# Softmax maxima carried by small DMAs and heads turned by VectorE, in a four-layer hybrid network

## The chip, the cores and the metric

One core of a Trainium2 chip runs the whole network in one launch. The metric is the device time of one execution in microseconds (us). The engines are TensorE (PE), which multiplies matrices and, with an identity, transposes; VectorE (DVE); ScalarE (ACT); GpSimd (POOL); and SyncE (SP), which here only issues DMAs. SBUF is the working memory of 128 partitions, PSUM the eight banks that TensorE writes.

## The reference

Sixteen images of 256 tokens and 128 channels pass four layers; all is float32. The change touches the second, and the first half of the third:

```
# L1: dense attention, 8 heads of D=16 (per image, 256 queries x 256 keys)
attn = softmax(einsum('bihd,bjhd->bijh', q, k) * D**-0.5, axis=2)
x = einsum('bijh,bjhd->bihd', attn, v).reshape(bs, n, 128) @ W_last.T + b_last + x
# L2: on layer-normed tokens, key j counts for query i where i-64 < j <= i
scores = where(valid, einsum('bnqd,bnkd->...', q, k) / sqrt(D), -1e30)
t = t + (softmax(scores) @ v).reshape(B, S, 128) @ Wo.T
t = t + experts(ln(t))        # top 2 of 16, mean form
```

Before them stands a spatial and channel gate (L0), after them a causal linear attention and experts with top 1 of 8 (L3).

## The kernel before

`attend` (L365) does both attentions in one loop. A tile n is one image: tiles 0 to 15 are dense, 16 to 31 windowed. A tile has four steps j=0 to 3, a step is two heads of one parity (the two heads that share a block of 32 partitions differ in parity, and the keys are kept in an even and an odd copy, in which the other head's 16 rows are zero). So there are 128 steps, s=4n+j. All engines walk the same steps, each in its own written order, and semaphores tie them; nothing is reordered by a scheduler.

In step s TensorE runs `by_query(s)` (L569): scores with queries on partitions, into one pair of PSUM banks. VectorE's `maximum(s)` (L832) takes each query's negated row maximum from them. The next by_query overwrites the banks and so waits for `max_ready`; in a windowed tile `mask_scores` (L616) goes ahead of it and waits. Five steps later (LAG), t=s-5, TensorE makes the scores again with keys on partitions (`by_key(t)`, L586), ScalarE takes the exponential (L755) into `prob`, and in windowed tiles GpSimd cuts out what lies outside the window (L496, L500). `weigh` (L639) multiplies with the values at j=1 and j=3 of a later tile; a column of ones in the values gives the softmax sums.

How the maximum comes to the other orientation: at j=3 VectorE's `split_max` (L846, L848) writes a tile's maxima as a high and a low part into `parts`, TensorE turns them at the next j=0 (`turn_max`, L624), ScalarE copies them (`take_max`, L748), and in each later step four matmuls `less_maximum` (L578) add them to the key scores:

```
for block in blocks:
    for i in range(2): less_maximum(i, block)   # pick x maxT, start=True
    for i in range(2): mm = by_key(i, block)    # start=False, stop=True
```

How the heads come out: ScalarE copies them from PSUM (`take_heads`, L762), TensorE turns them at j=0 (`turn_heads`, L652, four transposes), VectorE divides at j=1 (L854 reciprocal, L860 twice), TensorE turns back at j=2 (`turn_normed`, L659), ScalarE copies (`take_normed`, L769), and TensorE applies the output weight at the next j=0 (`project_out`, L668). VectorE adds the residual (`add_out`, L870) and measures the rows for the layer norm (L876, L882). Other work in the steps: `project` (L535) makes the next tile's queries and keys at j=2; ScalarE takes the query (L733, L736) and the even key (L741), VectorE the odd key (`take_odd`, L807); `project_v` (L544) and `take_values` (L822, L824) make the values; `turn_rows` (L676) and `gate_logits` (L688) serve the layers after. VectorE's expert choice (`choose`, L1553 and after) runs in steps of the last tiles. SyncE writes finished windowed rows to a table (L472).

Of the kernel before, what the change touches and what calls it, by code (L numbers as in the profile page):

```python
# [364 lines left out]
def attend(nc, xf, tokens, rows, table, weights, consts, q_bias, key_scales, v_bias, o_bias, pick, window_mask, gate,  # L365
# [22 lines left out]
    with stage(nc, "attend") as (sb, sem):  # L388
        query = sb("query", [128, 3, N])
        key = sb("key", [128, 3, 2, N])  # L390
        negmax = sb("negmax", [128, 2, 2, 4, 2])
        parts = sb("parts", [128, 2, 128], FP32R)
        maxT = sb("maxT", [128, 2, N], FP32R)
        vaug = sb("vaug", [128, 3, 2, 2, 4, 32])
        prob = sb("prob", [128, 2, 4, 2 * 512])
        heads = sb("heads", [128, 2, 2, 128])
        recip = sb("recip", [128, 16])
        normed = sb("normed", [128, 2, 128])
# [20 lines left out]
        high_max = sem("high_max")  # L419
        parts_ready = sem("parts_ready")  # L420
        max_turned = sem("max_turned")
        maxT_ready = sem("maxT_ready")
# [5 lines left out]
        heads_ready = sem("heads_ready")  # L428
# [3 lines left out]
        normed_turned = sem("normed_turned")  # L432
# [31 lines left out]

        with nc.Block() as block:
            @block.sync
            def _(sp):
                sp.wait_ge(zero_row_set, 1)
                sp.dma_start(table[0:1, :], zero_row[:]).then_inc(table_written, 16)
                for k in range(IMAGES):  # L470
                    sp.wait_ge(rows_ready, IMAGES + k + 1)
                    sp.dma_start(table[1 + N * k:1 + N * (k + 1), :].rearrange("(a p) c -> p a c", p=128),  # L472
                                 rows[:, 2 * k:2 * k + 2, 0:C]).then_inc(table_written, 16)
                sp.wait_ge(table_written, 16 * (IMAGES + 1))

            @block.gpsimd
            def _(pool):
                nc.gpsimd.memset(zero_row[:], 0.0).then_inc(zero_row_set, 1)
                nc.gpsimd.memset(parts[:].bitcast(FP32), 0.0).then_inc(zeros_set, 1)
# [44 lines left out]
            def _(pe):  # L524
                def project(n):
                    if n >= 1:
                        pe.wait_ge(query_ready, n)
                        pe.wait_ge(odd_ready, n)
                    if windowed(n):
                        pe.wait_ge(rowsT_ready, n - IMAGES + 1)  # L530
                        pe.wait_ge(vaug_ready, n)
# [18 lines left out]
                def score_pairs(s):  # L550
# [13 lines left out]
                    def by_query(i, piece):  # L564
# [4 lines left out]
                        return nc.tensor.matmul(ps[:, SCORE + i, at:at + width], query[rows, n % 3, a * 128:(a + 1) * 128],  # L569
                                                key[rows, n % 3, odd, from_:from_ + width], start=not windowed(n),  # L570
                                                stop=not windowed(n) or a == 1)

                    def less_maximum(i, block):
                        n, m = t // 4, t % 4
                        groups, odd = tiles(m)
                        rows = slice(32 * groups[i], 32 * groups[i] + 32)
                        b, from_, width, at = block
                        nc.tensor.matmul(ps[:, KEY_SCORE + i, at:at + width], pick[rows, odd, :],  # L578
                                         maxT[rows, n % 2, from_:from_ + width], start=True, stop=False)

                    def by_key(i, block):
# [6 lines left out]
                                                query[rows, n % 3, from_:from_ + width], start=False, stop=True)  # L588
# [30 lines left out]
                def turn_max(n):  # L619
                    pe.wait_ge(parts_ready, n + 1)  # L620
                    if n - 6 >= IMAGES:
                        pe.wait_ge(logits_taken, n - 5 - IMAGES)
                    for a in range(2):
                        mm = nc.tensor.transpose(ps[:, MISC, a * 128:(a + 1) * 128], parts[:, a].bitcast(FP32), ident)  # L624
                    mm.then_inc(max_turned, 1)

                def weigh(n, g):
                    if g == 0:
                        pe.wait_ge(vaug_ready, n + 1)
                        if n >= 1:  # L630
                            pe.wait_ge(heads_ready, n)
# [11 lines left out]

                def turn_heads(n):
# [1823 lines left out]
```

## Time and profile before

| | us |
|---|---|
| median of 3 runs | 893.64 (893.03 to 894.1) |
| profiled execution, its own time | 893.71 |
| its span | 892.0 |
| TensorE busy | 735.9 (83%) |
| VectorE busy | 606.4 (68%) |
| ScalarE busy | 422.3 (47%) |
| GpSimd busy | 421.5 (47%) |

The span runs from the first to the last record of the profiled execution; the execution's own time holds a little more around it. Busy shares are means over the whole network, which has stages with different limits; the stage in question runs from by_query at 79 us to about 453. A row of the timeline is one instruction, or several alike in a row (x4: from the first one's start to the last one's end); rows can overlap, since matmuls are pipelined and those on different blocks of 32 partitions run beside each other.

### The profile page before, as it was taken

What the parts mean: (1) busy time and instruction counts of PE and PEld (TensorE: products, weight loads), DVE (VectorE), ACT (ScalarE), POOL (GpSimd) and SP (SyncE); (2) the same over time, 40 slices, a digit from 0 to 9 for tenths busy, and PEclk for the clock granted to TensorE, in tenths of its full rate; (3) what the DMA queues carried; (4) which work ended last, traced back from release to release, by engine and by line L of the source; (5) the groups of instructions that cost most, each with busy time, mean ns of one, the idle gap of its engine ahead of it and who ended that gap; (6) DMA issues with size and microseconds to landing.
All of it is one profiled execution on the core that took longest, in us unless ns stands there. A gap on an engine that the chain in (4) does not pass through costs nothing. (4 is left out here: it accounts for less than half of the span.)

```text
span 892.0 us, 22133 instructions
## 1 busy us (share of the span) xinstructions
PE 735.9 (83%) x7941; PEld 571.1 (64%) x7941; DVE 606.4 (68%) x1583; ACT 422.3 (47%) x861; POOL 421.5 (47%) x560
## 2 busy tenths in 40 slices
PE   0659899999999999999864898866699888539994
PEld 0235566666667777777653787854467666439993
DVE  3765667777766666677469888867557777647774
ACT  0454555555554444444344566650466666124442
POOL 0336012222226776766820777730555687825551
PEclk9979999999999999999875899996799999659996
DMA  5830000000000000000000111140700000122216
GB/s 170 253 124 1 1 2 1 2 3 1 2 3 1 3 19 14 14 14 14 19 13 3 49 54 55 52 27 0 217 2 2 8 17 20 40 72 74 62 50 189
DMA packets 38222, 37.19 MB, mean 42 GB/s; under 512 B 4851, under 2 KB 30440, under 8 KB 38116
## 3 DMA queue, kind: packets, MB, share of 16 engines
q1 hardware_dynamic: 31204, 24.28, 9.2%
q0 software_dynamic: 4800, 9.40, 4.5%
q10 hardware_dynamic: 2112, 2.10, 0.7%
q8 instruction: 66, 1.08, 0.5%
q14 instruction: 40, 0.33, 0.1%
HBM read 26.76 MB, written 9.46 MB: 41 GB/s over the span
## 5 line engine op out<-in xcount | busy, mean ns | idle before, releaser
L832 DVE TENSOR_REDUCE attend_negmax<-ps 128x4 f32<-128x1024 f32 (+1 forms) x128 | 139.8, 1092 | 91.3 <-PE ps L569 90.8
L755 ACT ACTIVATE attend_prob<-ps 128x1024 f32<-128x1024 f32 (+1 forms) x128 | 110.6, 864 | 160.3 <-PE ps L586 160.0
L569 PE MATMUL ps<-attend_key,attend_query 32*128 32x256 f32 (+2 forms) x1024 | 124.8, 360 | 7.5 <-DVE attend_negmax L832 7.4
L586 PE MATMUL ps<-attend_query,attend_key 32*128 32x256 f32 (+2 forms) x1024 | 127.1, 343 | 0.0
L569 PEld LDWEIGHTS ps<-attend_key,attend_query 32*128 32x128 f32 x1024 | 79.5, 184 | 48.1 <-issue 46.4
L1817 POOL DMA_INDIRECT sums_xs<-table,sums_source x79 | 77.1, 976 | 56.8 <-DVE sums_source L1750 33.0
L578 PE MATMUL ps<-attend_maxT,pick 32*128 32x256 f32 (+2 forms) x512 | 100.2, 387 | 0.5 <-ACT attend_prob L755 0.5
L1535 PE MATMUL ps<-sums_xT,sums_own 128*128 128x128 f32 x632 | 84.2, 280 | 0.0
L1535 PEld LDWEIGHTS ps<-sums_xT,sums_own 128*128 128x128 f32 x632 | 78.5, 195 | 0.0
L586 PEld LDWEIGHTS ps<-attend_query,attend_key 32*128 32x128 f32 x1024 | 77.9, 185 | 0.3
L506 POOL TENSOR_SCALAR attend_rstd<-attend_spread 128x2 f32<-128x2 f32 x32 | 7.4, 231 | 142.5 <-DVE attend_spread L882 142.5
L1878 ACT ACTIVATE sums_hidden<-ps 128x512 f32<-128x512 f32 x79 | 47.2, 598 | 34.9 <-PE ps L1535 33.5
L496 POOL TENSOR_SCALAR_AFFINE_SELECT attend_prob<-attend_prob 128x512 f32<-128x512 f32 x64 | 41.0, 641 | 45.9 <-ACT attend_prob L755 45.9
L2050 POOL DMA_INDIRECT outputs<-expert_y,expert_token x39 | 37.9, 971 | 49.0 <-DVE expert_y L2156 45.1
L639 PE MATMUL ps<-attend_prob,attend_vaug 128*32 128x256 f32 (+2 forms) x1024 | 58.3, 345 | 0.6 <-POOL attend_prob L500 0.6
L1888 DVE TENSOR_REDUCE partial<-sums_hidden 128x4 f32<-128x512 f32 x79 | 53.9, 682 | 5.6 <-ACT sums_hidden L1878 2.3
L1282 ACT ACTIVATE linear_prob<-ps 128x1536 f32<-128x1536 f32 x32 | 46.2, 1443 | 16.6 <-PE ps L1150 16.6
L513 POOL TENSOR_SCALAR rows<-tokens,attend_spread,attend_rstd 128x128 f32<-128x128 f32 x64 | 50.7, 801 | 3.3
L578 PEld LDWEIGHTS ps<-attend_maxT,pick 32*128 32x128 f32 x512 | 47.9, 183 | 1.6 <-ACT attend_prob L755 1.4
L1083 POOL TENSOR_SCALAR_AFFINE_SELECT linear_prob<-linear_prob 128x1024 f32<-128x1024 f32 x32 | 35.0, 1094 | 28.0 <-ACT linear_prob L1282 27.9
L1524 DVE COPY sums_own<-w1T 128x512 f32 x79 | 34.6, 438 | 16.3 <-PE ps L1535 10.5
L2141 ACT ACTIVATE expert_hidden<-expert_before 128x512 f32<-128x512 f32 x39 | 24.6, 630 | 41.8 <-DVE expert_before L2182 41.8
(356 smaller groups left out, 1764.2 us busy)
## 6 DMA issues: line engine op xcount, KB each, us to landing
w<-in_L_ffn_w SPq DMA_DIRECT2D x1, 4096.0 KB, 27.7
expert_xs<-slots SPq DMA_DIRECT2D x39, 64.5 KB, 1.8
x<-in_x ACTq DMA_DIRECT2D x4, 512.0 KB, 8.0
table<-rows SPq DMA_DIRECT2D x16, 128.0 KB
experts<-in_L_ffn_W SPq DMA_DIRECT2D x1, 2048.0 KB, 8.5
experts<-in_L_ffn_W SPq DMA_DIRECT2D x4, 512.0 KB, 10.3
rows<-outputs SPq DMA_DIRECT2D x8, 256.0 KB, 5.1
out<-expert_result SPq DMA_DIRECT2D x8, 256.0 KB, 2.6
```

Of the source, the lines that this page charges most:

```text
L513: last = nc.gpsimd.tensor_scalar(rows[:, t, 0:C], tokens[:, t, :], spread[:, n % 2, a, 0:1], rstd[:, n % 2, a:a + 1], ALU.subtract, ALU.mult)
L569: return nc.tensor.matmul(ps[:, SCORE + i, at:at + width], query[rows, n % 3, a * 128:(a + 1) * 128], key[rows, n % 3, odd, from_:from_ + ...
L578: nc.tensor.matmul(ps[:, KEY_SCORE + i, at:at + width], pick[rows, odd, :], maxT[rows, n % 2, from_:from_ + width], start=True, stop=False)
L586: return nc.tensor.matmul(ps[:, KEY_SCORE + i, at:at + width], key[rows, n % 3, odd, b * 128:(b + 1) * 128], query[rows, n % 3, from_:from ...
L639: mm = nc.tensor.matmul(ps[32 * r:32 * r + 32, HEADS, c:c + width], vaug[:, n % 3, b, g, r, :], of_pair(n, 2 * g + r // 2)[:, r % 2, at:at ...
L755: nc.scalar.activation(of_pair(t // 4, t % 4)[:, :, 0:wide], ps[:, KEY_SCORE:KEY_SCORE + 2, 0:wide], ACT.Exp).then_inc(prob_ready, 1)
L832: last = nc.vector.tensor_reduce(out=negmax[:, s // 4 % 2, :, r:r + 2, odd].rearrange("p a r -> p r a"), in_=ps[:, SCORE:SCORE + 2, 0:2 * ...
L1282: nc.scalar.activation(prob[:, s % 2, :, 0:384], ps[:, SCORE:SCORE + 4, 0:384], ACT.Copy).then_inc(prob_ready, 1)
L1535: mm = nc.tensor.matmul(ps[:, bank + r % 2, c * 128:(c + 1) * 128], own[:, r % ring, c * 128:(c + 1) * 128], xT[:, r % 4, :], start=True, ...
L1817: nc.gpsimd.indirect_dma_start(out=xs[:, s % RING, :], out_offset=None, in_=table[:, :], in_offset=bass.IndirectOffsetOnAxis(ap=source[:, ...
L1878: nc.scalar.activation(hidden[:, r % 2, :], ps[:, UP + r % 2, :], ACT.Silu).then_inc(hidden_ready, 1)
L1888: nc.vector.tensor_reduce(out=partial[:, bass.ds(s, 1), :].rearrange("p s c -> p (s c)"), in_=hidden[:, r % 2, :].rearrange("p (c n) -> p ...
```

## The change

Two things change in `attend`, and one in how its keys are taken.

The maxima. The query is now held twice (`query[128, 3, 2, N]`), once per parity, with the other parity's 16 rows zero. Of these 16 unused rows one is used to carry the negated maximum, and the key's matching row holds 1, set by a bias as the key is taken; by_key then gives scores less maximum in one product, and less_maximum is gone. To get a maximum into that row, VectorE turns each step's four columns of maxima in 32x32 blocks (`turn_max(s)`, each step, after the step's other VectorE work), and SyncE moves them with four DMAs of 1x4x32 numbers (`place_max(s)`). by_key waits for `max_placed`. When by_query reads the same copy, before its maximum exists, that row still holds the zeros with which the query was taken.

The heads. VectorE turns them from PSUM in 32x32 blocks (`turn_heads`, j=0), inverts the sums (j=1), multiplies (`normalise`, one operation on two SBUF tiles, j=2) and turns back (`turn_normed`, j=3). TensorE's and ScalarE's parts of this are gone.

The odd key is taken by ScalarE. Waits follow: `project` waits for `vaug_ready` from tile 1 on, `turn_rows` for `rowsT_ready`.

```diff
@block.sync
-                for k in range(IMAGES):
+                def place_max(s):
+                    n, m = s // 4, s % 4
+                    groups, odd = tiles(m)
+                    sp.wait_ge(max_turned, s + 1)
+                    for i in range(2):
+                        row = free_row(groups[i], odd)      # 32 * group + 16 * (1 - odd)
+                        for a in range(2):
+                            sp.dma_start(query[row:row + 1, n % 3, odd, a * 128:(a + 1) * 128],
+                                         negmaxT[2 * a + i::32, s % 4, :]).then_inc(max_placed[s % 4], 16)
...
+                for s in range(4 * (COUNT + 7)):
+                    if s < SLOTS:
+                        place_max(s)
+                    if s % 4 == 0 and IMAGES <= s // 4 - 6 < COUNT:
+                        write_rows(s // 4 - 6 - IMAGES)
@block.tensor
-                        if t % 4 == 0:
-                            pe.wait_ge(maxT_ready, t // 4 + 1)
+                        pe.wait_ge(max_placed[t % 4], 64 * (t // 4 + 1))
                         if t >= 1:
                             pe.wait_ge(prob_ready, t)
                         for block in blocks:
-                            for i in range(2):
-                                less_maximum(i, block)
                             for i in range(2):
                                 mm = by_key(i, block)
@block.scalar
+                    for odd in range(2):
+                        took = nc.scalar.activation(query[:, n % 3, odd, :], ps[:, PROJECT, 0:N], ACT.Identity,
+                                                    scale=query_scale[:, odd:odd + 1],
+                                                    bias=query_scale[:, 2 + odd:3 + odd])
...
                     if j == 3 and runs(n + 1):
                         take_query(n + 1)
                         take_even(n + 1)
+                        take_odd(n + 1)
@block.vector
+                def turn_max(s):
+                    dve.wait_ge(max_ready, s + 1)
+                    if s >= 4:
+                        dve.wait_ge(max_placed[s % 4], 64 * (s // 4))
+                    nc.vector.transpose(negmaxT[:, s % 4, :], negmax[:, s % 2, :]).then_inc(max_turned, 1)
+
+                def turn_heads(n):
+                    dve.wait_ge(weighted, 2 * n + 2)
...
+                    nc.vector.transpose(headsT[:].rearrange("p g k d -> p (g k d)"), ps[:, HEADS, :])\
+                        .then_inc(heads_turned, 1)
...
+                    nc.vector.tensor_tensor(normed[:].rearrange("p k (g d) -> p g k d", g=2), headsT[:, :, :, 0:16],
+                                            recip[:, :, :, None].to_broadcast([128, 2, 8, 16]), ALU.mult)\
+                        .then_inc(normed_ready, 1)
```

On TensorE, in a dense tile in the middle of the run, steps j=1 and j=2 stand so before (L569 by_query, L578 less_maximum, L586 by_key, L639 weigh, L535 project, L676 turn_rows, L659 turn_normed):

```order
L569 MATMUL ps<-attend_key,attend_query 128x256 x4
L578 MATMUL ps<-attend_maxT,pick 128x256 x2
L586 MATMUL ps<-attend_query,attend_key 128x256 x2
L578 MATMUL ps<-attend_maxT,pick 128x256 x2
L586 MATMUL ps<-attend_query,attend_key 128x256 x2
L639 MATMUL ps<-attend_prob,attend_vaug 32x256 x8
L569 MATMUL ps<-attend_key,attend_query 128x256 x4
L578 MATMUL ps<-attend_maxT,pick 128x256 x2
L586 MATMUL ps<-attend_query,attend_key 128x256 x2
L578 MATMUL ps<-attend_maxT,pick 128x256 x2
L586 MATMUL ps<-attend_query,attend_key 128x256 x2
L535 MATMUL ps<-xf,wqk 128x256 x2
```

And so afterwards, from j=0 to j=2 (L586 is now by_query, L596 by_key, L561 project_v, L649 project_out, L638 weigh, L552 project, L658 turn_rows):

```order
L586 MATMUL ps<-attend_key,attend_query 128x256 x4
L596 MATMUL ps<-attend_query,attend_key 128x256 x4
L561 MATMUL ps<-wv,xf 128x128 x2
L649 MATMUL ps<-wo,attend_normedT 128x128 x2
L586 MATMUL ps<-attend_key,attend_query 128x256 x4
L596 MATMUL ps<-attend_query,attend_key 128x256 x4
L638 MATMUL ps<-attend_prob,attend_vaug 32x256 x8
L586 MATMUL ps<-attend_key,attend_query 128x256 x4
L596 MATMUL ps<-attend_query,attend_key 128x256 x4
L552 MATMUL ps<-xf,wqk 128x256 x2
L658 MATMUL ps<-const_all,rows 128x128 x2
```

The four less_maximum matmuls are gone from each step and no transpose of heads is left; the rest keeps its place.

On VectorE the same tile from j=1 to j=3 before (L832 maximum, L854 and L860 the division, L876 and L882 the row measures, L846 and L848 split_max, L807 take_odd):

```order
L832 TENSOR_REDUCE attend_negmax<-ps 128x2x2
L854 RECIPROCAL attend_recip<-ps 128x16
L860 TENSOR_TENSOR attend_normed<-ps,attend_recip 128x2x4x16 x2
L832 TENSOR_REDUCE attend_negmax<-ps 128x2x2
L876 BN_STATS attend_stats<-tokens 128x6 x2
L882 BN_AGGR attend_spread<-attend_stats 128x2 x2
L832 TENSOR_REDUCE attend_negmax<-ps 128x2x2
L846 CAST attend_parts<-attend_negmax 128x8x2
L848 TENSOR_TENSOR attend_parts<-attend_negmax,attend_parts 128x8x2
L807 TENSOR_SCALAR attend_key<-ps,key_scale 128x256
```

And afterwards from j=2 to j=0 (L782 maximum, L809 normalise, L831 and L837 the row measures, L792 turn_max, L817 turn_normed, L798 turn_heads, L825 add_out):

```order
L782 TENSOR_REDUCE attend_negmax<-ps 128x2x2
L809 TENSOR_TENSOR attend_normed<-attend_headsT,attend_recip 128x2x8x16
L831 BN_STATS attend_stats<-tokens 128x6 x2
L837 BN_AGGR attend_spread<-attend_stats 128x2 x2
L792 STREAM_TRANSPOSE attend_negmaxT<-attend_negmax 128x32
L782 TENSOR_REDUCE attend_negmax<-ps 128x2x2
L817 STREAM_TRANSPOSE attend_normedT<-attend_normed 128x256
L792 STREAM_TRANSPOSE attend_negmaxT<-attend_negmax 128x32
L782 TENSOR_REDUCE attend_negmax<-ps 128x2x2
L798 STREAM_TRANSPOSE attend_headsT<-ps 128x512
L825 TENSOR_TENSOR tokens<-tokens,ps 128x256
L792 STREAM_TRANSPOSE attend_negmaxT<-attend_negmax 128x32
```

The division moved from j=1 to j=2, ahead of the row measures, and each step ends with a transpose between its own maximum and the next.

## Rows read from the trace of the kernel before

**Rows 1.** Stretches: start:end, us, busy (instructions) by engine, clock, DMA share, GB/s.

```profile
92.90:103.00 10.10, 7.64 (x93) 5.48 (x92) 6.26 (x10) 6.33 (x9) 0.00 (x0) 1.00 0.00 0
150.12:161.12 11.00, 10.63 (x137) 7.57 (x135) 7.91 (x18) 6.34 (x10) 2.53 (x4) 1.00 0.01 1
```

**Rows 2.** Timeline, TensorE, dense tile: start, duration, engine, line, out<-in [idle before].

```profile
154.19 0.48 PE L569 MATMUL ps<-attend_key,attend_query 32*128 32x256 f32 x2 [0.19 <-DVE attend_negmax L832]
...
156.68 0.60 PE L652 MATMUL ps<-const_all,attend_heads 128*128 128x128 f32 x4
...
159.79 0.48 PE L569 MATMUL ps<-attend_key,attend_query 32*128 32x256 f32 x2 [0.18 <-DVE attend_negmax L832]
...
162.30 0.38 PE L659 MATMUL ps<-const_all,attend_normed 128*128 128x128 f32 x2
```

**Rows 3.** Timeline, TensorE and VectorE, a dense step early in the stage.

```profile
94.13 1.23 DVE L832 TENSOR_REDUCE attend_negmax<-ps 128x4 f32<-128x1024 f32 x1 [0.61 <-PE ps L569]
...
95.50 0.48 PE L569 MATMUL ps<-attend_key,attend_query 32*128 32x256 f32 x2 [1.12 <-DVE attend_negmax L832]
...
96.68 1.23 DVE L832 TENSOR_REDUCE attend_negmax<-ps 128x4 f32<-128x1024 f32 x1 [1.32 <-PE ps L569]
```

**Rows 4.** Timeline, ScalarE, the even key in that dense tile.

```profile
162.66 0.56 ACT L741 ACTIVATE attend_key<-ps,key_scale 128x256 f32<-128x256 f32 x1
```

**Rows 5.** Timeline, all engines, a windowed tile's steps j=2 and j=3.

```profile
292.13 0.38 PE L569 MATMUL ps<-attend_key,attend_query 32*128 32x128 f32 x2
...
293.02 0.96 DVE L832 TENSOR_REDUCE attend_negmax<-ps 128x4 f32<-128x768 f32 x1 [0.70 <-PE ps L569]
...
294.04 0.64 POOL L496 TENSOR_SCALAR_AFFINE_SELECT attend_prob<-attend_prob 128x512 f32<-128x512 f32 x1 [1.00 <-ACT attend_prob L755]
...
294.94 0.38 PE L569 MATMUL ps<-attend_key,attend_query 32*128 32x128 f32 x2
...
297.28 0.38 PE L569 MATMUL ps<-attend_key,attend_query 32*128 32x128 f32 x2
```

**Rows 6.** Timeline, TensorE: first windowed step, last step, last weigh, last project_out.

```profile
253.60 0.38 PE L569 MATMUL ps<-attend_key,attend_query 32*128 32x128 f32 x2
...
424.25 0.38 PE L569 MATMUL ps<-attend_key,attend_query 32*128 32x128 f32 x2
...
439.58 0.75 PE L639 MATMUL ps<-attend_prob,attend_vaug 128*32 128x192 f32 x16 [0.65 <-POOL attend_prob L500]
...
445.01 1.22 PE L668 MATMUL ps<-wo,attend_normedT 128*128 128x128 f32 x4 [0.80 <-ACT attend_normedT L769]
```

**Rows 7.** VectorE groups by line: shapes, count | busy us, mean ns | idle before.

```profile
L1888 DVE TENSOR_REDUCE partial<-sums_hidden 128x4 f32<-128x512 f32 x79 | 53.9, 682 | 5.6 <-ACT sums_hidden L1878 2.3
...
L870 DVE TENSOR_TENSOR tokens<-tokens,ps 128x256 f32<-128x256 f32 x32 | 13.2, 412 | 9.7 <-PE ps L668 9.7
...
L1555 DVE TENSOR_TENSOR choice_scratch<-choice_scratch,const_all 128x128 f32<-128x128 f32 x8 | 2.2, 279 | 0.2
```

**Rows 8.** Timeline, VectorE and GpSimd: row measures, and split_max beside a select.

```profile
151.11 0.48 DVE L876 BATCH_NORM_STATS2 attend_stats<-tokens 128x6 f32<-128x128 f32 x2
151.62 0.25 DVE L882 BATCH_NORM_AGGREGATE attend_spread<-attend_stats 128x2 f32<-128x6 f32 x2
...
296.85 0.65 POOL L496 TENSOR_SCALAR_AFFINE_SELECT attend_prob<-attend_prob 128x512 f32<-128x512 f32 x1 [1.47 <-ACT attend_prob L755]
...
297.04 0.49 DVE L848 TENSOR_TENSOR attend_parts<-attend_negmax,attend_parts 128x16 fp32r<-128x16 f32 x1
```

**Rows 9.** One line's instructions: count, shortest/median/longest ns, first and last start.

```profile
L848 DVE TENSOR_TENSOR attend_parts<-attend_negmax,attend_parts x32: 175/243/490, 90.2 to 426.3; 128x16 fp32r<-128x16 f32 x32
```

**Rows 10.** Timeline, SyncE's DMA issues at the kernel's start.

```profile
2.20 0.75 SPq L2297 DMA_DIRECT2D w_wv_r<-in_L_conv_wv_r  x1
...
12.23 0.43 SPq L2312 DMA_DIRECT2D gate_bias<-in_L_ffn_bs  x1
```

**Rows 11.** DMA issues by name: count, KB each, median us to landing.

```profile
expert_xs<-slots SPq DMA_DIRECT2D x39, 64.5 KB, 1.8
```

More of the change, by code:

```diff
@@ L418, in attend @@
         max_ready = sem("max_ready")
-        high_max = sem("high_max")
-        parts_ready = sem("parts_ready")
         max_turned = sem("max_turned")
-        maxT_ready = sem("maxT_ready")
+        max_placed = [sem(f"max_placed{r}") for r in range(4)]
         key_scored = sem("key_scored")
@@ L463, in tiles, with free_row @@
             return (2 * (m % 2), 2 * (m % 2) + 1), m // 2
+        def free_row(group, odd):
+            return 32 * group + 16 * (1 - odd)
         with nc.Block() as block:
@@ L568, in by_query @@
                         a, from_, width, at = piece
-                        return nc.tensor.matmul(ps[:, SCORE + i, at:at + width], query[rows, n % 3, a * 128:(a + 1) * 128],
+                        return nc.tensor.matmul(ps[:, SCORE + i, at:at + width],
+                                                query[rows, n % 3, odd, a * 128:(a + 1) * 128],
                                                 key[rows, n % 3, odd, from_:from_ + width], start=not windowed(n),
                                                 stop=not windowed(n) or a == 1)
[L573 to L579, printed above, removed]
                     def by_key(i, block):
@@ L587, in by_key @@
                                                 key[rows, n % 3, odd, b * 128:(b + 1) * 128],
-                                                query[rows, n % 3, from_:from_ + width], start=False, stop=True)
+                                                query[rows, n % 3, odd, from_:from_ + width], start=True, stop=True)
                     pieces, blocks = PIECES[windowed(s // 4)], BLOCKS[windowed(t // 4)]
@@ L617, in mask_scores @@
                                              window_mask[:, 128:512], start=True, stop=False)
[L619 to L625, printed above, removed]
                 def weigh(n, g):
@@ L701, in _ @@
                     if j == 0:
-                        if runs(n - 1):
-                            turn_max(n - 1)
                         if runs(n):
@@ L707, in _ @@
                             project_out(n - 4)
-                        if runs(n - 3):
-                            turn_heads(n - 3)
                     if j == 1 and runs(n - 2):
@@ L718, in _ @@
                             turn_rows(n - 5)
-                        if runs(n - 3):
-                            turn_normed(n - 3)
                     if j == 3 and runs(n - 2):
@@ L784, in _ @@
                 take_even(0)
+                take_odd(0)
                 for s in range(4 * (COUNT + 7)):
                     n, j = s // 4, s % 4
-                    if j == 0 and runs(n - 3):
-                        take_heads(n - 3)
                     if j == 3 and runs(n + 1):
```

179 lines of the change are left out of this document (66 added, 113 removed).

## The prediction

> **What bounds the kernel now.** I read first the stretches of the attention stage, engine by engine. In one dense tile of 11.00 us TensorE is busy 10.63, VectorE 7.91, ScalarE 6.34 [rows 1]; in a tile's length at the start, when weigh, turn_heads and turn_normed do not run yet, TensorE is busy 7.64 of 10.10 at granted clock 1.00 [rows 1]. So TensorE is full in the steady state, and what leaves it can count, until something else is full.
>
> What comes next is read in the timeline. There is one pair of score banks, so by_query (L569) of a step waits for the row maximum (L832) of the step before. Where TensorE has nothing more to do, this loop is seen alone: by_query at 95.50, maximum at 96.68 (1.18 later) for 1.23, and by_query 0.14 after a maximum's end (94.13+1.23=95.36, then 95.50) [rows 3]. That is 2.55 a step, and the two maxima stand 2.55 apart. Four steps are 10.20; the tile takes 11.00 because step j=0, where turn_heads starts 2.49 after by_query (154.19, 156.68) and runs 0.60, and j=2, where turn_normed starts 2.51 after by_query (159.79, 162.30) and runs 0.38, stand beyond 2.55 [rows 2]. Those tails are what this change removes.
>
> In the windowed half the loop is shorter: by_query to maximum 0.89 (292.13, 293.02), maximum 0.96, and the mask matmuls before the next by_query. Step j=3 took 2.34 (294.94, 297.28), step j=2, which TensorE overfills, 2.81 (292.13, 294.94) [rows 5].
>
> **The change, term by term.** All sums go against the profiled execution: 893.71 us, its span 892.0 and 1.7 around it; the median 893.64 is 0.07 below, which I ignore.
>
> *Dense steps.* From the seventh by_query (95.50) to the first windowed one (253.60) there are 58 steps in 158.10 us [rows 3, 6], 2.73 each. TensorE loses less_maximum in all steps, turn_max and turn_heads in j=0, turn_normed in j=2. Even with the others left in, j=0 ends at 2.49 and j=2 at 2.51 [rows 2]; both are below 2.55, so the loop is the floor, unless VectorE overfills it.
>
> VectorE may work 2.55-1.23=1.32 between two maxima. No row shows a 32x32-block transpose. The nearest row reads 128x512 in one pass in 0.682 (L1888) [rows 7]. As bounds I set one half, 0.34, and double, 1.36, and take 0.68, since the tile has that row's size. For the 128x32 turn_max I take 0.18, the shortest L848, with its longest, 0.49, as bound [rows 9]. Step j=0 is then 0.68+0.41 (add_out, L870 [rows 7])+0.18=1.27 and fits. In j=1, take_values and the reciprocal are at most 0.41+0.41+0.25 by larger rows [rows 7, 8], with turn_max 1.25: fits. In j=2 stand normalise, one operation of L870's size, 0.41, the row measures 0.76 (151.11 to 151.62+0.25 [rows 8]), turn_max 0.18 and 0.06 of gaps: 1.41, that is 0.09 over. In j=3 a 128x256 transpose of at most 0.68 fits. A tile is 10.20+0.09=10.29, a step 2.57: 58 x 2.57=149.2. **Gain 8.9.**
>
> ScalarE gains a second query and the odd key, 0.56 each at most like the even key at 162.66 [rows 4]. With them the exponential of j=3 starts at 162.66+3x0.56=164.34 and ends 1.02 later at 165.36; by_query of the next j=0 would start at 159.79+5.19=164.98, and by_key stands 0.25 behind it. So by_key is at worst 0.13 late, in a step whose TensorE work is the 2.49 less turn_max and less_maximum. I cost it at nothing; if that cover is gone it is 0.13 in each tile, 4 us.
>
> *Windowed steps.* 63 steps from 253.60 to 424.25 take 170.65 [rows 6]. I take j=1 and j=3 as 2.34, j=0 as 2.44 (its mask has the wide form, whose weight load stands before it; by the rows it lies between 2.34 and 2.81). VectorE's room is 2.34-0.96=1.38 and 1.48; the 1.27 and 1.25 fit. In j=2 something new collides. GpSimd's causal select starts 1.91 after by_query (294.04) and runs 0.64 [rows 5]; the maximum ends at 0.89+0.96=1.85, and normalise, which now reads two SBUF tiles instead of PSUM and SBUF, starts there. The trace shows what then happens: L848, two SBUF inputs, takes 0.18 at best but 0.49 at 297.04, while GpSimd's select runs from 296.85 to 297.50 [rows 8, 9]. I take a stall of 0.54, between nothing and the select's whole 0.65: the step is 1.85+0.54+0.41+0.76+0.18-0.89=2.85. A tile is 2.44+2.34+2.85+2.34=9.97; sixteen less the last step are 157.2. In about five tiles the expert choice adds an operation of 0.28 (L1555 [rows 7]) to each step, which no longer all fits: 0.5 a tile, 2.4. Together 159.6: **gain 11.0.**
>
> The Trainium skill, *SBUF — State Buffer*, section "Who interferes with whom", states that a VectorE instruction with two SBUF inputs and a GpSimd instruction that reads SBUF hold each other up, the later one waiting until the first is through. It speaks against this change, since normalise did not fall under it before; the trace agrees (0.18 and 0.49). By it step j=2 stays near 2.85; without it the step would be 2.44 and the total some 6 us lower, near 865.
>
> *Drain.* After the last weigh (439.58+0.75=440.33) project_out starts at 445.01, 4.68 later [rows 6], through two engines' changes for each turn. Afterwards there are VectorE's 0.68, 0.25, 0.41 and at most 0.41 in a row, and some 0.75 of hand-overs: 2.5. **Gain 2.2.** The stage's start, where the first steps have no keys to compute, I take as even.
>
> *What is added at nothing.* SyncE issues four DMAs a step, 512 in all, and by_key waits for their landing. Its twenty issues from 2.20 to 12.23 stand 0.53 apart [rows 10]; four are 2.11, below the shortest step, 2.34. The maximum is used five steps later: 5x2.34=11.7 after by_query; 2.2 to 2.9 go until it is turned, 2.1 into issuing, so over 6 us remain for landing, against 1.8 in the nearest row [rows 11] and bounds of nothing and some three times that. The rows of windowed tiles written to HBM share that queue, one DMA in four steps, 0.53 more; the slack above covers it.
>
> Sum: 8.9+11.0+2.2=22.1, **871.5 us**; without neighbours' cases the forecast's own range is 865 to 880 (transposes up to 0.9, a stall of 0 to 0.65).
>
> The Trainium skill, *Vector Engine (DVE) Microarchitecture Reference*, §3.8 "The reshape front-end and per-opcode configuration", states that the transpose is pipelined to one element per cycle and lane. No run here shows it yet; by it the dear case below falls away and the sum stands.
>
> **The rivals.**
>
> *Dear transposes.* If a block transpose takes two passes, turn_heads is 1.36 and j=0 on VectorE 1.95, 0.63 over in the dense half: the tile is 10.20+0.63+0.09=10.92, a step 2.73, gain 0. In the windowed half 0.47 a tile more, 7.5: gain 3.5; drain 1.2. Total 889. For it: no row shows the operation. Against: nothing in the rows makes one pass over such a tile dearer than 0.68.
>
> *Slower: SyncE cannot feed the maxima.* Each step needs four issues in order. At the longest row, 0.75 and 0.04 to the next [rows 10], a step takes 3.16; the 121 steps from 95.50 to 424.25 take 382 instead of 328.75, plus 53: 947. It decides from 328.75/121/4=0.68 an issue. The late form is landing: beyond some 6 us, each microsecond delays one in five steps' worth, about 24 us over 121 steps. For it: 0.53 is not far from 0.59, where it would use up a 2.34 step. Against: the small copies in the rows all start within 0.8 of each other.
>
> *The clock.* TensorE gets more gaps. Rows 1 show 76% busy at clock 1.00, and the tile afterwards is no emptier, since it has weigh in it. If the clock did fall to 1.2 GHz, 7.64 of work would be 15.3, 5 us more in a tile; the gain is gone after four of 32 tiles.
>
> *TensorE stays full.* If the matmul timings in the records hide more than they show, j=0 and j=2 keep their length; then only the drain is gained: 888 to 895. Against: the 2.49 and 2.51 are starts of instructions.
>
> *Better.* No stall and a shorter loop: 860 to 865.
>
> **How the numbers follow.** Forecast (865 to 880) 0.66; dear transposes 0.13; SyncE slower 0.10; clock 0.03; TensorE full 0.04; better 0.04. A measurement of this kernel tells about 0.2% from no change, 1.8 us. Faster: 0.66+0.04+most of the dear case, 0.12=0.82; the rest of that case and of the full TensorE are the 0.06 within; slower 0.12. The range reaches from 863 to 890, over the forecast, half of "better" and most of the dear case; the slower one lies outside.
>
> **What would show it.** By_query starts 2.55 apart in dense tiles, 10.2 to 10.4 a tile; VectorE's transposes at most 0.7 (128x512) and 0.2 (128x32); TensorE near 85% busy in a tile and the releaser of its gaps the maximum, not the DMA; in windowed j=2 a normalise near 0.95 instead of 0.41; SyncE's queue under 90% busy and by_key never released by a DMA; 2.5 from the last weigh to project_out. I am wrong if by_key waits for max_placed, if a dense tile stays near 11, or if the span outside the stage moves.

## The result

The changed kernel takes 865.54 us (median of 4, 864.95 to 866.61) against 893.66 for the kernel before in the same runs; the ratio is 0.9687, 95% interval 0.967 to 0.9704. It is 28.1 us faster; 22.1 were predicted (871.5, range 863 to 890). Its profiled execution took 864.95, the span 863.2.

Where the span's 28.8 us went, by landmarks of both traces (VectorE's maxima, and TensorE's first matmul of the next stage):

| stretch | before | after | gain | predicted |
|---|---|---|---|---|
| to the first maximum | 80.23 | 80.95 | -0.7 | 0 |
| 64 dense steps, to the first windowed maximum | 174.26 | 162.64 | 11.6 | 8.9 (of 58 steps) |
| 63 windowed steps, to the last maximum | 170.65 | 152.40 | 18.3 | 11.0 |
| drain, to the next stage | 28.47 | 28.54 | -0.1 | 2.2 |
| the rest | 438.39 | 438.67 | -0.3 | 0 |

VectorE's groups after the change, by shape (x count | busy us, mean ns | idle before); they answer to [rows 7, 9]:

```profile
L792 DVE STREAM_TRANSPOSE attend_negmaxT<-attend_negmax 128x32 f32<-128x32 f32 x128 | 22.8, 178 | 0.3
L798 DVE STREAM_TRANSPOSE attend_headsT<-ps 128x512 f32<-128x512 f32 x32 | 22.6, 706 | 5.8 <-PE ps L638 5.8
L817 DVE STREAM_TRANSPOSE attend_normedT<-attend_normed 128x256 f32<-128x256 f32 x32 | 13.9, 434 | 0.0
L809 DVE TENSOR_TENSOR attend_normed<-attend_headsT,attend_recip 128x256 f32<-128x256 f32 x32 | 13.7, 429 | 0.0
```

The transposes cost 0.178, 0.434 and 0.706, where 0.18, at most 0.68, and 0.68 were taken. From 256 to 512 columns the price rises by 0.272, 1.06 ns a column (the source also changes, from SBUF to PSUM). A row maximum, one pass over PSUM, rises by as much: 0.692 for 128x512 (in half_max below) and 1.224 for 128x1024 are 1.04 ns a column. The Trainium skill, *Vector Engine (DVE) Microarchitecture Reference*, §3.8 "The reshape front-end and per-opcode configuration", states one element per cycle and lane for the transpose; a price per column that equals a one-pass operation's agrees with that.

A dense tile of after, as in [rows 1, 3]: the stretch, then VectorE's maxima and TensorE's by_query (L586) in the timeline:

```profile
142.57:152.66 10.09, 9.50 (x114) 6.48 (x110) 8.08 (x19) 6.19 (x9) 2.53 (x4) 1.00 0.01 2
```

```profile
142.57 1.22 DVE L782 TENSOR_REDUCE attend_negmax<-ps 128x4 f32<-128x1024 f32 x1 [0.88 <-PE ps L586]
...
143.85 0.48 PE L586 MATMUL ps<-attend_key,attend_query 32*128 32x256 f32 x2
...
145.06 1.22 DVE L782 TENSOR_REDUCE attend_negmax<-ps 128x4 f32<-128x1024 f32 x1 [0.21 <-PE ps L586]
...
146.43 0.48 PE L586 MATMUL ps<-attend_key,attend_query 32*128 32x256 f32 x2 [0.25 <-DVE attend_negmax L782]
...
147.60 1.23 DVE L782 TENSOR_REDUCE attend_negmax<-ps 128x4 f32<-128x1024 f32 x1 [0.70 <-PE ps L586]
...
148.91 0.48 PE L586 MATMUL ps<-attend_key,attend_query 32*128 32x256 f32 x2
...
150.11 1.22 DVE L782 TENSOR_REDUCE attend_negmax<-ps 128x4 f32<-128x1024 f32 x1 [0.18 <-PE ps L586]
```

The tile is 10.09 instead of 11.00, at clock 1.00. Its steps from j=0 to j=3, by the maxima, are 2.49, 2.54, 2.51, 2.55. In j=1 TensorE waits for the maximum (0.25), in j=3 too (0.34 before 151.48); in j=0 and j=2 it hardly does, by_query follows 0.06 and 0.08 after the maximum's recorded end. So the loop is the floor of j=1 and j=3, and TensorE's own work, just as long, that of j=0 and j=2; half_max_odd below shows that part. TensorE's busy time, 9.50, is 94% of the tile and not the expected 85%. Records of matmuls overlap, and how much of the 9.50 is due to that no run here tells.

In windowed tiles the steps are 2.34 all round, except j=2, 2.37 in tiles 17 to 21 and 2.77 from tile 22, where gate_logits joins TensorE's j=2 (before: 2.81 and 3.21).

### The profile page after: what moved, and what is told of

The parts are those of the page before. It is cut to its first block and busy times, and to the rows that moved or that the text cites. A ratio compares the mean times of both kernels' runs of the same rounds, so it can differ in the third digit from the quotient of the medians.

```text
span 863.2 us, 21250 instructions
## 1 busy us (share of the span) xinstructions
PE 688.5 (80%) x7173; PEld 521.9 (60%) x7173; DVE 612.1 (71%) x1648; ACT 418.2 (48%) x829; POOL 424.5 (49%) x560
## 5 line engine op out<-in xcount | busy, mean ns | idle before, releaser
L782 DVE TENSOR_REDUCE attend_negmax<-ps 128x4 f32<-128x1024 f32 (+1 forms) x128 | 139.6, 1090 | 82.9 <-PE ps L586 82.2
L729 ACT ACTIVATE attend_prob<-ps 128x1024 f32<-128x1024 f32 (+1 forms) x128 | 110.7, 865 | 137.2 <-PE ps L596 137.2
L586 PE MATMUL ps<-attend_key,attend_query 32*128 32x256 f32 (+2 forms) x1024 | 124.8, 360 | 12.8 <-DVE attend_negmax L782 11.6
L596 PE MATMUL ps<-attend_query,attend_key 32*128 32x256 f32 (+2 forms) x1024 | 124.6, 359 | 1.1 <-ACT attend_prob L729 1.0
L586 PEld LDWEIGHTS ps<-attend_key,attend_query 32*128 32x128 f32 x1024 | 79.6, 184 | 53.5 <-issue 45.7
L596 PEld LDWEIGHTS ps<-attend_query,attend_key 32*128 32x128 f32 x1024 | 88.3, 184 | 2.3 <-issue 2.2
L638 PE MATMUL ps<-attend_prob,attend_vaug 128*32 128x256 f32 (+2 forms) x1024 | 58.8, 348 | 0.7 <-POOL attend_prob L516 0.6
L512 POOL TENSOR_SCALAR_AFFINE_SELECT attend_prob<-attend_prob 128x512 f32<-128x512 f32 x64 | 45.0, 702 | 24.7 <-ACT attend_prob L729 24.7
L516 POOL TENSOR_SCALAR_AFFINE_SELECT attend_prob<-attend_prob 128x512 f32<-128x512 f32 x64 | 40.8, 637 | 4.4
L1495 PE MATMUL ps<-expert_xT,expert_own 128*128 128x128 f32 x312 | 42.4, 280 | 0.0
```

Source lines behind the costliest of these rows:

```text
L512: nc.gpsimd.affine_select(out=causal, in_=causal, pattern=[[0, 2], [0, 2], [1, 128]], base=0, channel_multiplier=-1, compare_op=ALU.is_ge, ...
L596: return nc.tensor.matmul(ps[:, KEY_SCORE + i, at:at + width], key[rows, n % 3, odd, b * 128:(b + 1) * 128], query[rows, n % 3, odd, from_ ...
L638: mm = nc.tensor.matmul(ps[32 * r:32 * r + 32, HEADS, c:c + width], vaug[:, n % 3, b, g, r, :], of_pair(n, 2 * g + r // 2)[:, r % 2, at:at ...
L729: nc.scalar.activation(of_pair(t // 4, t % 4)[:, :, 0:wide], ps[:, KEY_SCORE:KEY_SCORE + 2, 0:wide], ACT.Exp).then_inc(prob_ready, 1)
L782: last = nc.vector.tensor_reduce(out=negmax[:, s % 2, 0:4].rearrange("p (a r) -> p r a", a=2), in_=ps[:, SCORE:SCORE + 2, 0:2 * width].rea ...
L1495: mm = nc.tensor.matmul(ps[:, bank + r % 2, c * 128:(c + 1) * 128], own[:, r % ring, c * 128:(c + 1) * 128], xT[:, r % 4, :], start=True, ...
```

## The experiments

The diffs are shortened to the lines that carry the change; some comments in them are mine. Those of heads_alone and maxima_alone are shown against the kernel before.

**Each part alone.** `heads_alone` is the kernel before with the heads' new way and the odd key on ScalarE; `maxima_alone` is the changed kernel with the heads' old way.

```diff
# heads_alone
-                        if runs(n - 3): turn_heads(n - 3)     # TensorE, j=0; turn_normed, j=2; ScalarE's copies
+                        if runs(n - 3): turn_heads(n - 3)     # VectorE, j=0; normalise j=2, turn_normed j=3
# maxima_alone
-                            for i in range(2): less_maximum(i, block)
+                        pe.wait_ge(max_placed[t % 4], 64 * (t // 4 + 1))
```

> The heads' way of the change (and the odd key on ScalarE), with the maxima's old way: split_max, turn_max, take_max and less_maximum stay. Theory (the loop of by_query and maximum is the floor, and each part alone clears most of what stood above it): steps j=0 go from 3.05 to about 2.55 in dense tiles and from 3.01 to about 2.5 in windowed ones, j=2 from 2.85 to 2.55 and from 2.81 to 2.55 (late windowed tiles 3.21 to 2.95); about 10 us in the dense half and 12 in the windowed one: 871. The rival, that the time follows TensorE's busy time: six transposes a tile are 0.98 us of matmul records against 3.1 for less_maximum (100.2 us in 32 tiles), so a quarter of the gain: 887.

> The maxima's way of the change (and the odd key on ScalarE), with the heads' old way: take_heads, six transposes on TensorE, two take_normed copies stay. Theory of the floor: less_maximum is worth about 0.25 us of a step's length and turn_max 0.27, so j=0 goes from 3.05 to about 2.53 and j=2 from 2.85 to 2.6, windowed alike: 871, and with the run of the heads alone the two gains add up to far more than the whole change's 28. The rival (busy time): three quarters of the gain, 872, but then the heads alone give 887 and the gains add up.

Measured: 880.15 (ratio 0.9838, 0.9809 to 0.9868) and 878.26 (0.9837, 0.9797 to 0.9877), gains of 13.5 and 15.4. Both expectations missed. That the two add up to 28.9, the whole change's 28, is partly chance, since the steps do not add up. By the maxima, steps j=0 and j=2 in dense tiles are 2.62 and 2.78 with the heads alone, 2.75 and 2.73 with the maxima alone, 2.49 and 2.51 with both: each part alone leaves TensorE above the loop's floor, and only both together bring it down to it. From 3.05, j=0 gains 0.43 by the heads, 0.30 by the maxima and 0.56 by both; from 2.85, j=2 gains 0.07, 0.12 and 0.34. Where heads_alone loses time, in the timeline around the start of a step j=2 (L568 by_query, L577 less_maximum, L534 project):

```profile
177.86 1.02 ACT L733 ACTIVATE attend_prob<-ps 128x1024 f32<-128x1024 f32 x1 [1.50 <-PE ps L585]
```

```profile
178.76 0.48 PE L568 MATMUL ps<-attend_key,attend_query 32*128 32x256 f32 x2
178.94 0.39 PE L577 MATMUL ps<-attend_maxT,pick 32*128 32x256 f32 x2
...
180.24 1.13 PE L534 MATMUL ps<-xf,wqk 128*128 128x256 f32 x4
...
181.52 0.48 PE L568 MATMUL ps<-attend_key,attend_query 32*128 32x256 f32 x2
```

The exponential ends at 178.88, and less_maximum starts 0.06 later, 0.18 behind by_query (0.03 in the kernel before); project then starts 1.48 after by_query instead of 1.33. There is one pair of key-score banks too, and with less_maximum in it this second loop is 2.52 long. I tested that by a shorter exponential:

```diff
# heads_half_exp
-                    wide = WIDE[windowed(t // 4)]
+                    wide = 256 if 8 <= t < 4 * IMAGES else WIDE[windowed(t // 4)]
```

> The heads alone, and in the dense tiles (from step 8 on) the exponential is taken of half of each head's key scores, so the outputs are not the reference's. In the run of the heads alone j=2 stayed at 2.78 where 2.55 was expected. Theory: there is a second loop, by_key to exponential to the next by_key, over the one pair of key-score banks; with less_maximum in it, it is 1.44+1.02+0.06=2.52, so by_key starts 0.18 behind by_query and project 0.17 later than in the kernel before. With an exponential of half the size (0.5 less) that delay goes: project at 1.33 after by_query instead of 1.50, j=2 2.61, total some 2 us below the heads alone. The rival, that the transposes left more on TensorE than their starts showed: 2.78 and the same total.

Measured: 875.6 (0.9802, 0.9785 to 0.9819), 4.5 below the heads alone where 2 was expected. Steps j=2 fell from 2.78 to 2.63, windowed ones stayed; by_query, less_maximum and project now stand so:

```profile
167.92 0.48 PE L568 MATMUL ps<-attend_key,attend_query 32*128 32x256 f32 x2 [0.18 <-DVE attend_negmax L792]
167.95 0.39 PE L577 MATMUL ps<-attend_maxT,pick 32*128 32x256 f32 x2
...
169.25 1.13 PE L534 MATMUL ps<-xf,wqk 128*128 128x256 f32 x4
```

0.03 and 1.33, as expected: the second loop is shown, and it is 0.15 of the 0.27 that j=2 loses when less_maximum goes too (2.78 to 2.51). The steps explain only some 2 of the 4.5: the dense steps take 2.0 less, but the first maximum of tile 28 stands at 369.24 instead of 370.76, since the stage began 0.4 later, and the rest lies behind this stage and stays open. With half the exponential the later layers work on other numbers.

**The loop after.** `half_max` shortens the maximum, `half_max_odd` also takes the odd key back to VectorE, `odd_on_vector` does only that.

```diff
# half_max: dense tiles
-   in_=ps[:, SCORE:SCORE + 2, 0:2 * width].rearrange("p r (a n) -> p r a n", a=2),
+   in_=ps[...].rearrange("p r (a n) -> p r a n", a=2)[:, :, :, 0:width if windowed(s // 4) else width // 2],
# odd_on_vector: ScalarE's take_odd(n + 1) goes; VectorE at j=3, behind turn_normed
+                        if runs(n + 1): take_odd(n + 1)
```

> The changed kernel; in the dense tiles VectorE takes the maximum over the first 128 of the 256 keys only, so what is subtracted is not the true maximum. Theory (after the change the loop of by_query and maximum is the floor of j=1 and j=3, 2.54, and TensorE's own work, 2.48, that of j=0 and j=2): a maximum of 0.68 instead of 1.22 frees j=1 and j=3 to about 2.3 and leaves j=0 and j=2, a dense tile goes from 10.09 to 9.55, total 857.5. The rival, that SyncE's DMAs or the exponential hold the steps: 865.5.

> The changed kernel with the odd key back on VectorE, at j=3 behind turn_normed. Theory (it is on no path: 0.53 fits into VectorE's room at j=3, 1.2 to 1.4 with 0.6 in it): 865.5 within 1. The rival, that ScalarE's longer j=3 holds by_key up, or that VectorE has no room: 3 us off in either direction.

> Half the maximum in dense tiles as in the run before, with the odd key back on VectorE. With half the maximum a dense tile fell to 9.91 only, since j=0 rose to 2.94: by_key waits there for the exponential of j=3, which stands behind two queries and two keys on ScalarE. Theory: with the odd key gone from ScalarE that exponential is 0.45 earlier, j=0 falls to about 2.5 and a tile to 9.5, total 856 to 858. The rival, that VectorE or SyncE holds j=0: 862.

Measured: odd_on_vector 866.1 (0.9695, 0.9671 to 0.9719), no difference, so that edit is free in the changed kernel. half_max 862.19 (0.9662, 0.9645 to 0.9678): j=1 and j=3 fell to 2.26 and 2.09, so the maximum did hold them, but j=0 rose to 2.94 and the tile stood at 9.91. Why, in half_max's timeline at the end of j=3 and the start of j=0 (L716, L721 the keys, L729 the exponential, L586 by_query, L596 by_key):

```profile
177.54 0.56 ACT L716 ACTIVATE attend_key<-ps,key_scale 128x256 f32<-128x256 f32 x1
...
177.99 0.57 ACT L721 ACTIVATE attend_key<-ps,key_scale 128x256 f32<-128x256 f32 x1
...
178.44 1.03 ACT L729 ACTIVATE attend_prob<-ps 128x1024 f32<-128x1024 f32 x1
...
178.83 1.13 PE L586 MATMUL ps<-attend_key,attend_query 32*128 32x256 f32 x8
...
179.62 1.13 PE L596 MATMUL ps<-attend_query,attend_key 32*128 32x256 f32 x8
```

by_key waits 0.79 behind by_query for an exponential that stood behind the keys. half_max_odd confirms it: 856.24 (0.9568, 0.9543 to 0.9592), j=0 2.55, a tile 9.52, as expected. There TensorE has no gap left, over 10 us of dense tiles (us, busy of PE, PEld, DVE, ACT, POOL, clock):

```profile
130.00:140.00 10.00, 10.00 (x115) 7.04 (x116) 7.05 (x22) 6.28 (x9) 2.53 (x4) 1.00 0.01 1
```

So 9.5 a tile is TensorE's own work, and the changed kernel's 10.09 stands 0.6 above it for the maximum's sake. ScalarE's cover for the odd key, costed at nothing, is real but only as wide as the loop is long.

**SyncE's DMAs.**

```diff
# fifth_dma, behind the four of place_max
+                    sp.dma_start(spare[0:1, s % 4, :], negmaxT[4:128:32, s % 4, :]).then_inc(max_placed[s % 4], 16)
-                        pe.wait_ge(max_placed[t % 4], 64 * (t // 4 + 1))
+                        pe.wait_ge(max_placed[t % 4], 80 * (t // 4 + 1))
# turn_max on VectorE waits for the fifth too
-                        dve.wait_ge(max_placed[s % 4], 64 * (s // 4))
+                        dve.wait_ge(max_placed[s % 4], 80 * (s // 4))
```

> The changed kernel with a fifth DMA of 512 bytes in each step, into a place that nobody reads, for which by_key waits as for the other four. Theory (SyncE's issues stand 0.536 us apart, 12 in 6.43; four are 2.14 of a step of 2.34, five are 2.68, more than any step): 640 issues take 343 us from 82.4, so the last maximum lands near 427 instead of 402, less the slack of some 6 us used up first; total 884 to 890, and by_key waits for the DMAs. The rival, that issues have room or overlap: at most 867.

Measured: 894.3 (1.0011, 0.9994 to 1.0027): one more DMA a step gives back the whole gain; the last maximum stands at 421.82 instead of 395.99, 25.8 of the 28.8. SyncE's queue, first of the changed kernel (16 issues of four steps, 9.27), then of this one:

```profile
315.31 9.27 SPq L477 DMA_DIRECT2D attend_query<-attend_negmaxT  x16
```

```profile
340.93 2.10 SPq L478 DMA_DIRECT2D attend_query<-attend_negmaxT  x4
343.07 0.49 SPq L480 DMA_DIRECT2D attend_spare<-attend_negmaxT  x1
343.61 2.10 SPq L478 DMA_DIRECT2D attend_query<-attend_negmaxT  x4
```

Five take 2.68, without a gap. The forecast of 884 to 890 was low by about 5: I had left out the issue for written rows (0.48 in each of some ten tiles). And the wait comes to light elsewhere than expected (waits from 200 to 430: total us, times, longest):

```profile
PE ps L598 <- DMA attend_spare<-attend_negmaxT: 5.3, 9, 1.0
...
DVE attend_negmaxT L794 <- DMA attend_spare<-attend_negmaxT: 37.0, 60, 1.8
```

Mostly turn_max waits, for its buffer of four steps before, and with it VectorE's next maximum; by_key's matmuls wait 5.3 and its weight loads 10.9.

**Normalise beside GpSimd.** The windowed j=2 of after, where a stall of 0.54 was predicted (VectorE and GpSimd):

```profile
286.75 0.96 DVE L782 TENSOR_REDUCE attend_negmax<-ps 128x4 f32<-128x768 f32 x1 [0.76 <-PE ps L586]
...
287.62 0.41 DVE L809 TENSOR_TENSOR attend_normed<-attend_headsT,attend_recip 128x256 f32<-128x256 f32 x1
287.64 0.89 POOL L512 TENSOR_SCALAR_AFFINE_SELECT attend_prob<-attend_prob 128x512 f32<-128x512 f32 x1
...
288.63 0.18 DVE L792 STREAM_TRANSPOSE attend_negmaxT<-attend_negmax 128x32 f32<-128x32 f32 x1
...
289.13 0.96 DVE L782 TENSOR_REDUCE attend_negmax<-ps 128x4 f32<-128x768 f32 x1 [0.31 <-PE ps L586]
```

Normalise came 0.02 before the select, so the select was held, 0.89 instead of 0.64. The Trainium skill, *SBUF — State Buffer*, "Who interferes with whom", states that the order of issue decides which of the two blocks; this row agrees, and so do those of the next run. I turned the order round:

```diff
# turn_max_first: VectorE at j=2
+                    if j == 2 and s < SLOTS: turn_max(s)
                     if j == 2 and runs(n - 3): normalise(n - 3)
-                    if s < SLOTS:
+                    if s < SLOTS and j != 2:
                         turn_max(s)
```

> The changed kernel with turn_max ahead of normalise in steps j=2, the same instructions. Theory: in windowed tiles normalise starts 0.02 ahead of GpSimd's select and it is the select that is held up (0.90 instead of 0.64); if normalise starts 0.17 later the select is first and normalise waits some 0.47, as the prediction had it; steps j=2 go from 2.37 to about 2.85 in tiles 17 to 21 and from 2.77 to 2.86 after: 3 us more, 868.5. The rival, that VectorE has room in that step whoever comes first: 865.5.

Measured: 865.43 (0.9682, 0.9655 to 0.9709), no difference. Its rows in the same place:

```profile
278.12 0.64 POOL L512 TENSOR_SCALAR_AFFINE_SELECT attend_prob<-attend_prob 128x512 f32<-128x512 f32 x1
...
278.22 0.21 DVE L792 STREAM_TRANSPOSE attend_negmaxT<-attend_negmax 128x32 f32<-128x32 f32 x1
...
278.35 0.68 DVE L809 TENSOR_TENSOR attend_normed<-attend_headsT,attend_recip 128x256 f32<-128x256 f32 x1
```

Now normalise is held, by 0.27, and the steps go from 2.37 to 2.40 only: the rival was right, VectorE had the room, and just so: 0.31 idle before the next maximum in the rows of after, 0.00 in this run's tiles 17 to 21.

**The drain.** The same edit in both kernels:

```diff
# light_drain_after, light_drain_before
+                    if t >= 122:
+                        causal, recent = both[:, :, :, 0:32], both[:, :, :, 64:96]
```

> The changed kernel; GpSimd's two selects of the last six steps cover 32 of their 128 columns, so the last windows are not fully cut out. From the last maximum to the last project_out the kernels before and after take the same, 19.9 and 19.8, where 2.2 less was predicted. Theory: GpSimd's chain of selects and row normalisation sets the end of the last weigh in both (14.4 and 14.7 after the last maximum), so a faster way of the heads comes into it only behind that. With the selects 5 us shorter the stretch falls by 3 to 5 in both kernels, and the changed one is then some 2 shorter than the one before. The rival, that the heads' way gains nothing because TensorE's clock falls earlier in the changed kernel: the two stretches stay alike.

> The kernel before with the same edit (the selects of the last six steps over 32 of 128 columns). Theory: last maximum to last project_out 16 to 17, against about 15 in the changed kernel with that edit. Rival: alike within 0.5.

From the last maximum to the last project_out: 17.58 in the kernel before, 15.85 in the changed one, where without the edit it is 19.87 and 19.83. In the changed kernel unedited (first two rows) and edited (last two):

```profile
410.72 1.29 PE L638 MATMUL ps<-attend_prob,attend_vaug 128*32 128x192 f32 x16 [0.62 <-POOL attend_prob L516]
...
415.82 1.22 PE L649 MATMUL ps<-wo,attend_normedT 128*128 128x128 f32 x4 [1.48 <-DVE attend_normedT L817]
```

```profile
410.95 0.75 PE L640 MATMUL ps<-attend_prob,attend_vaug 128*32 128x192 f32 x16 [0.22 <-POOL attend_prob L518]
...
414.99 1.22 PE L651 MATMUL ps<-wo,attend_normedT 128*128 128x128 f32 x4 [0.65 <-DVE attend_normedT L819]
```

The theory held in the main: 2.3 and 4.0 less, where 3 to 5 were expected, and the changed kernel is then 1.7 shorter. So GpSimd's selects do set the last weigh in the real kernels, 14.44 and 14.72 after the last maximum. But the 1.7 is not all the heads' way: 1.26 of it lies ahead of the last weigh's end (13.82 and 12.56 after the last maximum) and 0.47 behind it (3.76 and 3.29). And GpSimd is not all that hides it. From the last weigh's end to project_out the unedited kernels take 4.68 [rows 6] and 3.81, so 0.87 is gained there; it is lost again because the weigh starts 0.28 later and takes 1.29 instead of 0.75. That is the clock, so the rival named above is right in part: TensorE's granted clock fell from 1.00 (2.4 GHz) to 0.50 (1.2 GHz) 15.5 after the last maximum in the kernel before, behind the last weigh, and 11.9 after it in the changed one, ahead of it. In the 8.6 us ahead of its fall TensorE was busy 6.96 in the kernel before, in 8.4 us 6.64 in the changed one. The changed kernel behind the fall, then the one before ahead of it (us, busy of PE, PEld, DVE, ACT, POOL, clock):

```profile
407.90:417.00 9.10, 5.49 (x34) 4.06 (x34) 3.51 (x14) 0.77 (x2) 6.71 (x11) 0.50 0.10 30
```

```profile
432.00:440.60 8.60, 6.96 (x94) 5.19 (x93) 2.19 (x11) 3.36 (x9) 8.00 (x14) 1.00 0.05 15
```

With the light selects both last weighs run at 1.00 and take 0.75. Why 3.81 and not the predicted 2.5 stands in VectorE's rows of the changed kernel (L1511 and L1513 are the expert choice, as is L1515, left out):

```profile
412.08 0.72 DVE L798 STREAM_TRANSPOSE attend_headsT<-ps 128x512 f32<-128x512 f32 x1 [4.22 <-PE ps L638]
413.20 0.42 DVE L825 TENSOR_TENSOR tokens<-tokens,ps 128x256 f32<-128x256 f32 x1 [0.41 <-PE ps L649]
413.54 0.28 DVE L1511 TENSOR_REDUCE top<-logits 128x8 f32<-128x128 f32 x1
413.74 0.24 DVE L803 RECIPROCAL attend_recip<-attend_headsT 128x16 f32<-128x16 f32 x1
413.92 0.29 DVE L1513 TENSOR_TENSOR choice_scratch<-logits,top 128x128 f32<-128x128 f32 x1
414.13 0.42 DVE L809 TENSOR_TENSOR attend_normed<-attend_headsT,attend_recip 128x256 f32<-128x256 f32 x1
414.47 0.48 DVE L831 BATCH_NORM_STATS2 attend_stats<-tokens 128x6 f32<-128x128 f32 x2
414.98 0.25 DVE L837 BATCH_NORM_AGGREGATE attend_spread<-attend_stats 128x2 f32<-128x6 f32 x2
...
415.33 0.44 DVE L817 STREAM_TRANSPOSE attend_normedT<-attend_normed 128x256 f32<-128x256 f32 x1
```

The four operations of the heads do not run in a row: add_out, which waits 0.41 for project_out, three operations of the expert choice and the row measures stand between them in VectorE's written order.

The totals, 864.32 (0.9672, 0.9651 to 0.9692) and 892.07 (0.9989, 0.9969 to 1.0008), are 1.2 and 1.5 below those of their kernels, less than a total of this kernel tells. In the changed kernel's edit the profiled execution, 4.0 shorter behind the last maximum, had lost 3.2 ahead of it, where the edit changes nothing: it began 0.5 later, and the granted clock fell to 0.50 for 6.83 us in the dense steps:

```profile
102.23:109.06 6.83, 6.83 (x53) 4.01 (x49) 3.17 (x6) 2.05 (x2) 0.00 (x0) 0.50 0.01 1
```

**A version beyond it.**

```diff
# logits_j1: TensorE
+                    if j == 1 and runs(n - 6) and windowed(n - 6): gate_logits(n - 6)    # behind weigh
-                        if runs(n - 6) and windowed(n - 6): gate_logits(n - 6)           # j == 2
```

> The changed kernel with gate_logits moved from j=2 to j=1 on TensorE, behind weigh; the same work. Theory (late windowed steps j=2 are TensorE's, 2.77 against 2.37 in tiles without gate_logits, and j=1 has some 0.4 between weigh and the next mask): 9 tiles by 0.4, 862. The rival, that j=1 grows by what j=2 loses: 865.5.

Measured: 863.21 (0.968, 0.9655 to 0.9705). In tiles from 22 on j=1 rose from 2.34 to 2.44 and j=2 fell from 2.77 to 2.38, but in tiles 26, 28 and 30 only to 2.55: there VectorE has no gap before the next maximum, an operation of the expert choice stands in that step (0.65 at 345.64). The 63 windowed steps take 150.32 instead of 152.40, 2.1 less; the interval of the total does not set it apart from the changed kernel.

## Why the prediction came out

The time came out within the range, and the mechanism held: the loop, and the work taken off TensorE. Its size did not: by landmarks the dense half gave 2.7 and the windowed half 7.3 more than forecast, the drain 2.3 and the start 0.7 less, so misses of opposite sign partly cancelled.

- *The loop of by_query and maximum is the floor*: right for j=1 and j=3; shown by half_max, where they follow the maximum. In j=0 and j=2 TensorE's own work is about as long (half_max_odd).
- *"Even with the others left in, j=0 ends at 2.49 and j=2 at 2.51"*: wrong. Heads_alone has them in and takes 2.62 and 2.78. Two things were missed: the start of turn_heads is not where by_query could start instead (project_out at 175.64, by_query at 176.18 in that kernel, 2.58 after the last), and the second loop over the key-score banks. The sum survived since the change removes less_maximum as well; that the steps then measured 2.49 and 2.51 is chance.
- *Dense tile 10.29*: measured 10.09. j=2 on VectorE, "0.09 over", was 1.41 by adding recorded durations; from normalise's start to the next maximum's start the trace has 150.11-148.74=1.37 with 0.18 of it idle. Each instruction starts before the record of the one ahead has ended. The other 0.11 are steps j=0 and j=2, 0.04 to 0.06 under the loop's 2.55: by_query follows the maximum's recorded end there by 0.06 and 0.08, not by the 0.14 of the sum. Why, no run shows.
- *Windowed 11.0*: the mis-sized term, 18.3. Step j=2 was 2.37 and 2.77, not 2.85 (the stall fell on GpSimd, and turn_max_first shows that VectorE could have taken it: 5 tiles by 0.5, 10 by 0.1, 3 us), j=0 2.34 and not 2.44 (1.6), and the expert choice lengthened no step (2.4). The prediction's own numbers had normalise at 1.85 and the select at 1.91, so normalise first, and charged the stall to normalise all the same. That 2.77 is near 2.85 is chance: it is TensorE's, from gate_logits, as logits_j1 shows, and it also covers three steps that the expert choice would have brought to 2.55.
- *The Trainium skill's section "Who interferes with whom", by which j=2 was to stay near 2.85*: the interference is there, 0.25 and 0.27, but it costs a step only what exceeds VectorE's room; the total came out near the 865 that the prediction gave for the case without it.
- *Drain 2.2*: wrong, -0.1. The failed step is "in a row": VectorE's operations after the last weigh, with what stands between them, took 3.81 and not 2.5, and the 0.87 that this still gained went into a last weigh that started 0.28 later and ran at clock 0.50.
- *SyncE hidden, 0.53 an issue*: right, 0.536, and fifth_dma shows how narrowly. No by_key waited for a DMA in the changed kernel.
- *Start even*: 0.7 lost. The first by_query now stands behind two queries on ScalarE, which is 0.55 of it; 0.17 was lost ahead of this stage (read from the trace, not tested).

## What to carry to other kernels

Two engines that hand one bank pair back and forth make a floor that no removed work can undercut; look for every such pair (here scores with VectorE, key scores with ScalarE) and put its length beside the step before costing an edit. When adding up an engine's operations, go through everything that its written order puts between them. Work taken off a full engine is worth its time only down to that floor, and what two edits give together is read from the steps, not from the sum of their gains. When small DMAs replace matmuls, multiply the issue time by the count per step and compare it with the step: 2.14 of 2.34 went unnoticed, 2.68 cost everything.

## What was not expected of the hardware

A SyncE issue's time did not follow its size: one of 512 bytes took as long (0.49, 0.536 with the gap) as those of up to 192 KB at the kernel's start (0.53 apart). A VectorE instruction with two SBUF inputs and a GpSimd select that start 0.02 to 0.23 apart cost the later one 0.25 to 0.27, less than what was left of the earlier one (0.39 and 0.41). TensorE's granted clock, 1.00 (2.4 GHz) throughout the dense steps of the changed kernel, fell to 0.50 (1.2 GHz) for 6.83 us in those of light_drain_after, after 10.2 us in which TensorE was busy 7.41; three steps took 2.86, 3.99 and 3.13 instead of 2.55, 2.48 and 2.55. The two kernels do the same until then, and what made the difference no run shows.
